# ELU and second attention projection in one stage of a graph-network kernel

## The reference

```
h = gat_conv(x, s, d, W1, att_src1, att_dst1, b1, heads=8, out_c=16, concat=True)
h = jax.nn.elu(h)
out = gat_conv(h, s, d, W2, att_src2, att_dst2, b2, heads=1, out_c=128, concat=False)

# in gat_conv
xh = (x @ W).reshape(N, heads, out_c)
a_src = jnp.sum(xh * att_src, axis=-1)
a_dst = jnp.sum(xh * att_dst, axis=-1)
...
e = jnp.exp(alpha - m[dst])
s = jax.ops.segment_sum(e, dst, num_segments=N)
coef = e / s[dst]
msg = xh[src] * coef[:, :, None]
out = jax.ops.segment_sum(msg, dst, num_segments=N)
```

## Time and profile before

| | us |
|---|---|
| median of three runs | 2071.18 |
| the profiled execution | 2069.24 |
| its span in the trace | 2067.4 |
| VectorE's last instruction of `gat_nodes` (trace time) | 1430.51 |
| VectorE's last instruction of `gat_linear` | 1461.77 |

### The profile page before, as it was taken

The page is one execution under the profiler, slowest core; times in us unless marked ns, Lnnn a source line. Parts: engine busy times, 40 slices in busy tenths (PEclk is TensorE's granted clock), DMA queues, the critical chain, the costliest instruction groups (busy, mean ns, idle before and its releaser), DMA issues. The chain is left out here.

```text
span 2067.4 us, 56651 instructions
## 1 busy us (share of the span) xinstructions
PE 1640.1 (79%) x23014; PEld 1482.0 (72%) x23014; DVE 1481.0 (72%) x2364; ACT 1232.5 (60%) x1981; POOL 886.1 (43%) x559
## 2 busy tenths in 40 slices
PE   4599999964388882378888888881499799999996
PEld 1599999953376761377778777771499788898895
DVE  6788989834577774389999999984688644444545
ACT  1355666521255551298889988881367566666665
POOL 0699999801445542098888877700000000000000
PEclk9799999986699996589999999995799999999998
DMA  1100000002111211311110011103300000000001
GB/s 57 41 14 13 15 14 13 14 7 80 52 34 50 55 52 29 76 32 42 43 42 27 22 42 43 38 3 103 97 26 13 24 20 12 3 1 3 16 1 52
DMA packets 82632, 68.24 MB, mean 33 GB/s; under 512 B 21630, under 2 KB 74001, under 8 KB 82273
## 3 DMA queue, kind: packets, MB, share of 16 engines
q1 hardware_dynamic: 79047, 62.01, 10.4%
q0 software_dynamic: 3328, 2.56, 0.7%
HBM read 47.36 MB, written 17.19 MB: 31 GB/s over the span
## 5 line engine op out<-in xcount | busy, mean ns | idle before, releaser
L2251 ACT ACTIVATE branch_mask<-branch_row,att_att 128x3126 bf16<-128x3126 f32 (+1 forms) x208 | 461.0, 2289 | 46.5 <-DMA branch_row<-dst_row 38.7
L2564 PE MATMUL sage_acc<-sage_cr,sage_hl 128*128 128x448 f32 x1750 | 378.5, 372 | 10.3 <-DVE sage_hl L2680 10.3
L497 POOL DMA_INDIRECT swp_slab<-records,e_rows x100 | 314.4, 3144 | 89.7 <-POOLq L120 55.9
L2564 PEld LDWEIGHTS sage_acc<-sage_cr,sage_hl 128*128 128x128 f32 x1750 | 324.1, 189 | 35.7 <-DVE sage_hl L2680 10.4
L2328 PE MATMUL branch_acc<-branch_v,branch_mask 128*128 128x102 bf16 (+1 forms) x5000 | 299.7, 214 | 61.9 <-DVE branch_mask L2278 37.5
L2284 DVE TENSOR_TENSOR branch_mask<-branch_mask,k_C 128x3126 bf16<-128x3126 bf16 (+1 forms) x208 | 312.6, 1550 | 17.2 <-ACT branch_mask L2251 16.3
L2590 ACT ACTIVATE sage_cr<-k_C 128x896 fp32r<-128x896 bf16 x250 | 235.2, 945 | 146.8 <-PE sage_acc L2564 142.7
L2328 PEld LDWEIGHTS branch_acc<-branch_v,branch_mask 128*128 128x128 bf16 (+1 forms) x5000 | 256.7, 100 | 87.9 <-DVE branch_mask L2278 41.5
L2650 DVE CAST sage_cr<-k_C 128x896 fp32r<-128x896 bf16 x250 | 128.6, 515 | 207.2 <-PE sage_acc L2564 207.2
L2517 POOL TENSOR_TENSOR sage_xr<-sage_xr,sage_b 128x640 f32<-128x640 f32 x5 | 7.7, 1551 | 470.4 <-DMA sage_xr<-x 470.4
L419 PE MATMUL swp_pw<-swp_hot,swp_low_hot 128*128 128x100 bf16 x1568 | 198.9, 217 | 12.9 <-DVE swp_hot L413 9.8
(11 more groups left out here) (297 smaller groups left out, 2902.4 us busy)
## 6 DMA issues: line engine op xcount, KB each, us to landing
branch_row<-dst_row SPq DMA_DIRECT2D x24, 384.0 KB
mean_feat<-in_edge_attr SPq DMA_DIRECT2D x50, 144.0 KB, 2.2
branch_row<-dst_row SPq DMA_DIRECT2D x8, 411.0 KB
table<-lin_tab SPq DMA_DIRECT2D x5, 340.0 KB, 5.9
branch_tab<-table SPq DMA_DIRECT2D x8, 212.5 KB
att_sums<-branch_mask SPq DMA_DIRECT2D x8, 212.5 KB, 2.3
post_sums<-att_sums SPq DMA_DIRECT2D x5, 340.0 KB, 3.2
table<-lin_tab SPq DMA_DIRECT2D x5, 322.5 KB, 2.4
```

The costliest lines, as they stand in the source:

```text
L497: pool.indirect_dma_start(slab[:, t % 2, j * ROW:(j + 1) * ROW, :].rearrange("p e f -> p (e f)"), None, k.records, bass.IndirectOffsetOnAx ...
L2251: nc.scalar.activation(mask[:, slot(e, s), cols(lo, hi)], row[:, cols(lo, hi)], ACT.Relu, bias=g.att[:, 1, bass.ds(h + s * heads, 1)], sca ...
L2564: ins = pe.matmul(acc[:, bank, 0:hi - lo], hl[:, part, g % RING, :], cr[:, n % CR_SLOTS, lo - first:hi - first], start=g == 0 and part == ...
```

## The change

A new stage, `gat_middle` (tiles named `mid`), replaces `gat_nodes` of the first step and `gat_linear` of the second. A strip's rows stay in on-chip memory (three slots of `k.agg`) from the division to the transposition. The exponential of the negative part is taken on ScalarE in two steps, ReLU of the negated value and then the exponential of its negative; the subtraction of 1 moves into ScalarE's copy of the transposed strip as its bias. `w2 @ att` is computed once and appended to the weights as two columns, so a product with the 130-column weights gives the table row and both terms. ScalarE copies the products straight into a table kept on chip (`g2.tab`), which `scaled_sums` reads. `h`, `table2` and the transfers to and from them are gone.

```
+        with nc.Block() as block:
+            @block.sync
+            def _(sp):
...
+                load(0)
+                sp.dma_start(b[:, :], a["b1_2"].partition_broadcast(P)).then_inc(b_in, 16)
+                sp.dma_start(w[:, 0:D], a["w2_2"]).then_inc(w_in, 16)
+                with nc.allow_non_contiguous_dma(reason="one value per partition"):
+                    for j, n in enumerate(("att_src2", "att_dst2")):
+                        sp.dma_start(att[:, j:j + 1], a[n].rearrange("h c -> (h c)").rearrange("(c o) -> c o", o=1)
+                                     ).then_inc(att_in, 16)
+                for i in range(1, STRIPS):
+                    load(i)
...
+                def scaled(i):
+                    dve.wait_ge(sums_in[i], 16)
+                    link(dve.reciprocal(rw[:, i % 3, :], sums[:, i, :, :, hc:hc + 1].rearrange("p h t c -> p (h t c)")))
+                    if i > 2:
+                        dve.wait_ge(turned, i - 2)
+                    link(dve.tensor_tensor(y[:, i % 3].rearrange("p t (h c) -> p h t c", h=heads), sums[:, i, :, :, 0:hc],
...
+                    dve.tensor_tensor(y[:, i % 3], y[:, i % 3], mid(b[:, :], STRIP), ALU.add).then_inc(y_ready, 1)
+
+                def joined(i):
+                    dve.wait_ge(exps, i + 1)
+                    dve.scalar_tensor_tensor(out=y[:, i % 3], in0=y[:, i % 3], scalar=0.0, in1=below[:, i % 2],
+                                             op0=ALU.max, op1=ALU.add).then_inc(h_ready, 1)
+
+                def att_terms(i):
+                    dve.wait_ge(tab_ready, i + 1)
+                    for lo, hi, tiles in banks(i):
+                        ins = dve.tensor_copy(g2.att[:, 0:2, lo:hi], tiles[:, :, D:wide].rearrange("p t j -> p j t"))
+                    ins.then_inc(terms, 1)
+
+                scaled(0)
+                scaled(1)
+                for i in range(STRIPS):
+                    joined(i)
+                    if i + 2 < STRIPS:
+                        scaled(i + 2)
+                    if i:
+                        att_terms(i - 1)
+                att_terms(STRIPS - 1)
+                dve.wait_ge(terms, STRIPS)
+                dve.tensor_scalar(g2.att[:, 4, :], g2.att[:, 0, :], SLOPE, None, ALU.mult)
+
+            @block.scalar
+            def _(act):
...
+                def negative(i):
+                    act.wait_ge(y_ready, i + 1)
+                    if i > 1:
+                        act.wait_ge(h_ready, i - 1)
+                    nc.scalar.activation(below[:, i % 2], y[:, i % 3], ACT.Relu, scale=-1.0).then_inc(folded, 1)
+                    act.wait_ge(folded, i + 1)
+                    nc.scalar.activation(below[:, i % 2], below[:, i % 2], ACT.Exp, scale=-1.0).then_inc(exps, 1)
+
+                negative(0)
+                negative(1)
+                for i in range(STRIPS):
+                    act.wait_ge(turned, i + 1)
+                    if i > 1:
+                        act.wait_ge(xh, i - 1)
+                    nc.scalar.activation(xT[:, i % 2, :], pT[:, i % 2, 0:SW], ACT.Identity, bias=minus[:, :]
+                                         ).then_inc(xT_ready, 1)
+                    if i + 2 < STRIPS:
+                        negative(i + 2)
+                    act.wait_ge(xh, i + 1)
+                    for lo, hi, tiles in banks(i):
+                        ins = nc.scalar.activation(g2.tab[:, lo:hi, 0:D], tiles[:, :, 0:D], ACT.Copy)
+                    ins.then_inc(tab_ready, 1)
+
+            @block.tensor
+            def _(pe):
...
+                def turn(i):
+                    pe.wait_ge(h_ready, i + 1)
+                    if i > 1:
+                        pe.wait_ge(xT_ready, i - 1)
+                    for c in range(STRIP):
+                        ins = pe.transpose(pT[:, i % 2, c * P:(c + 1) * P], y[:, i % 3, c, :], k.ident[:, :])
+                    ins.then_inc(turned, 1)
+
+                turn(0)
+                pe.wait_ge(wa_ready, 1)
+                for i in range(STRIPS):
+                    if i + 1 < STRIPS:
+                        turn(i + 1)
+                    pe.wait_ge(xT_ready, i + 1)
+                    if i > 1:
+                        pe.wait_ge(terms, i - 1)
+                    for c in range(STRIP):
+                        ins = pe.matmul(pX[:, i % 2, at(c):at(c) + wide], xT[:, i % 2, c * P:(c + 1) * P], w[:, :],
+                                        start=True, stop=True)
+                    ins.then_inc(xh, 1)
...
@@ scaled_sums
                 load_row(0)
-                for i in range(STRIPS):
-                    load_tab(i)
                 load_row(1)
...
@@ attention_sums, program
-        gat_linear(nc, a, k, g)
+        if n == 1:
+            gat_linear(nc, a, k, g)
+        else:
+            g.tab = m.sb("tab", [P, TILES, D + 1], F32)
+            gat_middle(nc, a, k, before, g)
...
-            gat_nodes(nc, a, k, attention_sums(nc, a, k, 1, HEADS, k.x2, k.h))
+            g1 = attention_sums(nc, a, k, 1, HEADS, k.x2)
```

More of the change, by code:

```diff
@@ L1568, in gat_max @@
         m = Memory(nc, ctx, f"max{g.n}")
-        row = m.sb("row", [P, NP], F32)
+        row = m.sb("row", [P, NP], F32) if g.n == 1 else k.agg[:, 0:NP]
         far = m.sb("far", [P, 2, NP], BF16)
@@ L1798, in gat_sums @@
         m = Memory(nc, ctx, f"sum{g.n}")
-        tab = m.sb("tab", [P, TILES, w1], F32)
+        tab = m.sb("tab", [P, TILES, w1], F32) if g.n == 1 else g.tab
         if g.n == 1:
@@ L1952, in scaled_sums @@
         acc = m.ps("acc", [P, 2, 2 * BANK])
-        tab_in = [m.sem(f"tab_in{i}") for i in range(STRIPS)]
         row_in, x_in = ([m.sem(f"{n}{i}") for i in (0, 1)] for n in ("row_in", "x_in"))
@@ L2079, in step @@
                     def step(n, s, slot):
-                        if j == 0 and slot == 0:
-                            if isinstance(s, int):
-                                pe.wait_ge(tab_in[0], 16)
-                            else:
-                                for i in range(1, STRIPS):
-                                    pe.wait_ge(tab_in[i], 16)
                         pe.wait_ge(weights, n + 1)
                         for c in range(STRIP):
-                            ins = pe.matmul(acc_tile(j, c), e[:, slot, c * P:(c + 1) * P], one(tab, s),
+                            ins = pe.matmul(acc_tile(j, c), e[:, slot, c * P:(c + 1) * P], one(g.tab, s),
                                             start=isinstance(s, int) and s == 0 and c % per_bank == 0, stop=False,
@@ L2362, in load @@
                         sp.wait_ge(used, i - 1)
-                    sp.dma_start(sums[:, i % 2].rearrange("p h t c -> p h (t c)"),
-                                 g.sums[:, :, i * STRIP:(i + 1) * STRIP, :].rearrange("h p t c -> p h (t c)")
-                                 ).then_inc(sums_in[i % 2], 16)
-                    if not first:
-                        sp.dma_start(x[:, i % 2], strip_of(k.x2, i)).then_inc(x_in[i % 2], 16)
-                load(0)
-                sp.dma_start(b[:, :], a[f"b{g.n}_2"].partition_broadcast(P)).then_inc(consts, 16)
-                load(1)
-                for i in range(STRIPS):
-                    if i + 2 < STRIPS:
-                        load(i + 2)
-                    if first:
-                        sp.wait_ge(normed, i + 1)
-                        sp.dma_start(strip_of(g.out, i), out[:, i % 2]).then_inc(stored[i % 2], 16)
-                if first:
-                    for s in (0, 1):
-                        sp.wait_ge(stored[s], 16 * len(range(s, STRIPS, 2)))
+                    sp.dma_start(sums[:, i % 2], g.sums[0, :, i * STRIP:(i + 1) * STRIP, :]).then_inc(sums_in[i % 2], 16)
+                    sp.dma_start(x[:, i % 2], strip_of(k.x2, i)).then_inc(x_in[i % 2], 16)
+                load(0)
+                sp.dma_start(b[:, :], a["b2_2"].partition_broadcast(P)).then_inc(consts, 16)
+                for i in range(1, STRIPS):
+                    load(i)
             @block.scalar
@@ L2385, in _ @@
                     act.wait_ge(to_act, i + 1)
-                    if first:
-                        nc.scalar.activation(sq[:, :, :], sq[:, :, :], ACT.Exp).then_inc(from_act, 1)
-                    else:
-                        nc.scalar.activation(st[:, 2, :], st[:, 1, :], ACT.Sqrt).then_inc(from_act, 1)
+                    nc.scalar.activation(st[:, 2, :], st[:, 1, :], ACT.Sqrt).then_inc(from_act, 1)
             @block.vector
             def _(dve):
-                links = 3 if first else 3 + NORM_LINKS
-                if not first:
-                    dve.memset(k.mv[:, :, 0], 0.0)
-                    dve.memset(k.mv[:, :, 1], 1.0)
+                links = 3 + NORM_LINKS
+                dve.memset(k.mv[:, :, 0], 0.0)
+                dve.memset(k.mv[:, :, 1], 1.0)
                 dve.wait_ge(consts, 16)
@@ L2737, in _, with attention_sums @@
                                              in1=st[:, i % 2, 0, :], op0=ALU.mult, op1=ALU.mult).then_inc(shifted, 1)
```

(7 more changed lines are left out.)

110 lines of the change are left out of this document (68 added, 42 removed).

## The result

The changed kernel takes 2040.5 us (median of 4 runs, 2037.5 to 2045.5), the kernel before on the same chip 2072.0 (4 runs): a ratio of 0.9847, 95% interval 0.9828 to 0.9866. Forecast were 2044.4 us and 2038 to 2052. The profiled execution is the slowest of the four, 2045.5 us with a span of 2043.7.

What follows compares the result with a forecast made beforehand. Two short stages were taken as chains that fill no engine, 61.3 us in all; the new stage ending at 1436.0 against 1461.77 gains 25.8, the row load 1.0, so 2071.2 - 26.8 = 2044.4 us, range 2038 to 2052.

Steps and rivals of the forecast that it cites:

- Head: Start of the new stage: strip 0's ELU at 1409.6 us, set by the landing of strip 1's sums.
- the rule on columns of single elements: Attention column loads ahead of strip 1's sums: one descriptor per element, so strip 1 lands late, losing 1.2 us.
- Rounds: New stage's loop from strip 1's ELU to strip 4's: three rounds, each 5.8 us at low clock, 4.3 at full.
- Tail: New stage from strip 4's ELU on, nothing overlapping: 7.5 us at the full clock, 10.0 at the low one.
- Clock: TensorE in the new stage: two rounds at 1.2 GHz, the rest at 2.4.
- The rival of an early rise: New stage: clock rises with the first round or TensorE matters less; gain 28.8 + 1.0, 2041.4 us; chance 0.17.
- Row load: First row load of `scaled_sums`, without five table loads behind it: gains 1.0 us, between 0 and 1.0.
- Behind: Stages after the new one: unchanged but for the row load; a longer low clock in the weighted sum would cost 1.4.
- all rounds at the low clock: New stage: the clock never rises, as gaps break TensorE's stretches; gain 21.8 + 1.0, 2048.4 us; chance 0.25.
- The series: New stage: strips go through without overlap, some 8.7 us each; gain 14.7 + 1.0, 2055.5 us; chance 0.04.
- The slower case: Weighted sum loses the full clock: 38 us of low-clock products eat the gain, all make about 2145 us; chance 0.02.

Runs made afterwards that it cites:

- the first repeat: The changed kernel run again with nothing edited, against the kernel before: 2039.4 us, ratio 0.9854.
- the repeats: The changed kernel run again twice with nothing edited, against the kernel before: 2039.4 us (0.9854) and 2038.8 us (0.9848).
- the run with early loads: Changed kernel with strip 1's sums loaded third and ScalarE's exponentials of strip 0 ahead of its copies of the turned weights: 2040.0 us, 0.9847 of the kernel before.

## Why the prediction was right, and where its terms were off

The mechanism was the forecast one. The stage became one loop; from the first load to VectorE's last instruction it took 35.1, 32.5 and 32.7 us in the three traces, where 35.6 were forecast and 61.3 had been. That the first trace lies within 0.5 us of the forecast is luck in part: its head was 1.7 us longer than in the sum, its rounds 1.6 us shorter.

- **Head: too short.** Forecast 9.2 us to strip 0's ELU, measured 10.9, 10.1 and 10.0. Strip 1's division began 8.9, 7.9 and 7.9 us after the first load, not 7.0. In the first trace its load was asked for late, 4.6 us after the first one and not 3.4: the weights took 0.99 us to issue and the second column 1.65 where 0.45 stood in the sum, the bias 0.87 and not 1.60. In all three VectorE went on 4.2 to 4.5 us after the issue, not the 3.5 taken from the earlier trace rows, so near the slow end of 4.7 that stood for the rule on columns of single elements (the Trainium skill, "DMA: Bandwidth & Descriptors", "Rules for kernel authors"). The traces agree with the rule in the count of pieces: around the stage's loads the first repeat has 5520 packets under 512 bytes, the kernel with the terms on VectorE, which loads rows, 5264. They do not agree that the columns made the load late: without them it was 4.55 us, and in the run with 26 idle products at the stage's start, whose load stands ahead of the columns, 5.4.
- **Head: a term left out.** The sum has strip 0's exponentials done 8.1 us after the first load, hidden behind strip 1's division. They were done after 9.6, 10.0 and 10.0, for ScalarE's program has its table load (1.28 us) and two copies of the turned weights ahead of them, and the sum has no term for these. So strip 1's division alone moved everything only in the first trace; in the repeats ScalarE was as late, and in the run with early loads it was the last.
- **Rounds: a little too long.** 5.8 and 4.3 us forecast, 5.3 to 5.4 and 3.74 measured. Products, copy and ELU cost nearly what the sum says (2.38, 0.77, 0.81); the terms cost 0.15 to the next ELU's start where 0.27 were taken, the products start 0.2 us ahead of the end of the transposes, and the handovers are 0.12 together (0.06, 0.04 and 0.02 in the round shown), not 0.3.
- **Tail.** 7.5 forecast, 6.95 measured, for the same reasons.
- **Clock.** Two low rounds were forecast and came in one trace of the three; in the other two there was one. The rival of an early rise, with none, did not come. The same program does either, so the forecast could not have told them apart. That is 1.1 us on the mean of the three.
- **Row load.** 1.0 taken, between 0 and 1.0; measured 4.48 less 4.17, 3.88 and 3.75, so 0.3 to 0.7.
- **Behind.** From `bound_ones` to the end are 604.8 to 607.1 us in the three traces without the change and 604.2 to 605.7 in these three: nothing was lost in the weighted sum or the layers.

The account closes: the stage of 62.2, 62.8 and 63.3 us in the three traces without the change, 36.0, 33.4 and 33.6 with it, gives 28.4 on the means, and the row load some 0.6. That is 29 of the 30 to 31.5 us by which the medians differ. The rest is below the spread of the 1400 us ahead: the new stage began between 1394.5 and 1402.4 us in the eleven traces that have it. By the same means the 3.9 us of the median below the forecast are 2.1 of the stage (head +1.2, rounds -1.7, clock -1.1, tail -0.5), +0.4 of the row load, and some 2 that no term explains and that lie in that spread.

Of the 28.4 us, 17.8 hang on where the terms are formed, with what that does to tail and clock. The kernel with the terms on VectorE keeps the other 11 or so (51.4 against 62.2 to 63.3); no run splits them between the reload of `h`, the stage boundary, the two passes and the wait that are gone.

The rivals: all rounds at the low clock were seen in the kernel with the terms on VectorE, not in this one. The series would have shown rounds of 8.7 us; they were shorter by 3.3 and more. The slower case had nothing for it in the trace.

## What to carry to other kernels

Where two short stages with a reload between them become one, build the new one as a loop over the engines and look for what stands between one strip's step and the next on the in-order engine: there 0.15 us of copies in place of 3.3 us of sums gave 17.4 us, more than the 15 us of work that VectorE lost, for tail and clock moved with them. Moving even these copies one strip later made the stage 2.0 us shorter in the traces (the median 3.6 lower, with intervals that overlap). A wait that is removed uncovers the next (load, table load, division), so the trace is read again after every edit. Neither try at warming TensorE with idle products gained time: both times they put the turned weights later, and exponentials that stand behind these on ScalarE held up VectorE.

## What the runs showed of the hardware

- ScalarE's table load can stand behind the wait of the activation that needs it: in the new stage 20 us of idle time lay ahead of it, then came its 1.28 us, in the run with early loads on the path. In the kernel before it ran 6 us ahead of its exponential, and with a one-column exponential at the stage's start it did so in the new stage too. The Trainium skill, "ScalarE: Activation LUTs", "What ACT_TABLE_LOAD costs", gives about 1.28 us for the load and 1.38 for a drain. The load agrees, while the activation started 0.02 us behind it (1406.36 + 1.28 to 1407.66), so that no drain behind it is seen here.
- TensorE's clock can fall again soon after it rose. With 26 idle products at the stage's start it was at 1.00 from 1406 to 1410 and at 0.50 in 1412 to 1414, with 0.9 us of work in the 2 us between, so that the next products took 2.38 us. With the terms on VectorE it was at 1.00 from 1423 to 1426, while TensorE did nothing, and at 0.50 from 1427 on. With 12 and 14 in two places it stayed at 1.00 from 1402 to 1426, through 2 us with 0.29 us of work. Why one kept it and the others not is open.
- The issue of one and the same load on SyncE, that of the bias, took 0.87, 1.78 and 1.50 us in three traces of one program, and 0.58 to 2.01 us in all eleven traces of the new stage.
